# Three banks each for two kinds of attention scores, or two for one and four for the other

## The reference

```python
q = bitnet_linear(hidden_states, q_weight, q_scale)      # 32 heads of 32
k = bitnet_linear(hidden_states, k_weight, k_scale)      # 8 heads of 32, each used by 4 query heads
v = bitnet_linear(hidden_states, v_weight, v_scale)
scores = jnp.einsum('bhqd,bhkd->bhqk', q, k) / np.sqrt(HEAD_DIM)
attn = jax.nn.softmax(scores, axis=-1)
out = jnp.einsum('bhqk,bhkd->bhqd', attn, v)
...
x = x + bitnet_linear(out, o_weight, o_scale) + ffn(xn)
```

## Time and profile before

| | |
|---|---|
| median of 3 runs | 2635.26 us (2633.21 to 2635.6) |
| the profiled execution, its own time | 2635.6 us |
| its span in the trace | 2633.6 us |
| attention, from the first row scores to the last pair sums | about 315 to 1289 us |
| mean granted clock of PE over the span | 0.962 of full speed |
| busy: PE, DVE, ACT, POOL | 92%, 69%, 59%, 37% of the span |

### The profile page before, as it was taken

The page is one execution under the profiler, slowest core; times in us unless marked ns, Lnnn a source line. Parts: engine busy times, 40 slices in busy tenths (PEclk is TensorE's granted clock), DMA queues, the critical chain, the costliest instruction groups (busy, mean ns, idle before and its releaser), DMA issues.

```text
span 2633.6 us, 33630 instructions
## 1 busy us (share of the span) xinstructions
PE 2421.2 (92%) x12408; PEld 968.9 (37%) x12408; DVE 1828.4 (69%) x2362; ACT 1559.0 (59%) x1988; POOL 983.0 (37%) x545
## 2 busy tenths in 40 slices
PE   2499899989999999999689999999999999999998
PEld 1344322222222222222234444444444444444444
DVE  6756687766676767666154777777777777777777
ACT  3633267766676777667512666666666566666664
POOL 1000058788787888879600112122000112122000
PEclk9799889999999999999789999999999999999999
DMA  5100045544545455455412111112111311012211
GB/s 165 64 4 33 22 79 81 87 68 74 75 75 83 69 80 72 74 79 73 102 68 92 33 32 49 32 42 98 45 41 64 128 32 49 32 47 101 101 41 64
DMA packets 173711, 174.65 MB, mean 66 GB/s; under 512 B 87587, under 2 KB 119203, under 8 KB 173559
## 3 DMA queue, kind: packets, MB, share of 16 engines
q1 hardware_dynamic: 111286, 150.62, 18.2%
q0 software_dynamic: 62272, 22.03, 10.9%
HBM read 160.08 MB, written 65.45 MB: 86 GB/s over the span
## 4 chain that ended last, share of the span: by engine, by line
PE 54%; POOL 8%; issue 6%; DVE 1%; ACT 1%; DMA 1%; SPq 0%; DVEq 0%; POOLq 0%; ACTq 0%
PE ps L1309 29%; PE ps L1325 15%; POOL zone L504 6%; PE ps L1289 4%; PE ps L1212 2%; PE ps L1201 1%; POOL dequantised L525 1%; PE ps L1224 1%; PE ps L1185 1%; POOL zone L513 1%; PE ps L1341 0%; DMA zone<-in_L_attn_o_weight_dram 0%; ACT zone L657 0%; DVE zone L1098 0%; POOL zone L508 0%
## 5 line engine op out<-in xcount | busy, mean ns | idle before, releaser
L934 DVE TENSOR_REDUCE zone<-ps 128x1 f32<-128x512 f32 x1024 | 639.6, 683 | 271.5 <-PE ps L1185 271.3
L657 ACT ACTIVATE zone<-ps,sm 128x512 f32<-128x512 f32 x1024 | 631.6, 690 | 267.2 <-PE ps L1201 170.5
L1309 PE MATMUL ps<-xT,zone 128*128 128x512 f16 x3584 | 774.6, 379 | 3.6 <-DVE zone L1098 2.8
L504 POOL TENSOR_TENSOR zone<-zone 128x1024 f32<-128x1024 f32 x256 | 649.7, 2689 | 69.9 <-ACT zone L657 41.0
L1075 DVE TENSOR_SCALAR ps<-ps,zone_c 128x1024 f32<-128x1024 f32 x392 | 506.8, 1293 | 161.1 <-PE ps L1309 159.2
L725 ACT ACTIVATE ps<-ps,zone_c 128x1024 f32<-128x1024 f32 x392 | 426.8, 1089 | 261.1 <-PE ps L1309 259.3
L1309 PEld LDWEIGHTS ps<-xT,zone 128*128 128x128 f16 x3584 | 350.1, 98 | 427.4 <-DVE zone L1098 4.2
L1201 PE MATMUL ps<-zone 98*128 98x512 f16 x1024 | 392.9, 387 | 55.7 <-ACT zone L657 55.7
L1185 PE MATMUL ps<-zone 96*128 96x512 f16 x1024 | 405.2, 397 | 11.3 <-DMA zone<-zone 10.5
L1325 PE MATMUL ps<-zone 128*128 128x512 f16 x1792 | 387.1, 379 | 0.0
L1086 DVE TENSOR_SCALAR ps<-ps,zone_c 128x1024 f32<-128x1024 f32 x216 | 279.3, 1293 | 93.0 <-PE ps L1325 92.9
(11 more groups left out here) (127 smaller groups left out, 1292.6 us busy)
## 6 DMA issues: line engine op xcount, KB each, us to landing
zone<-dequantised SPq DMA_DIRECT2D x84, 512.0 KB, 3.6
dequantised<-zero_points SPq DMA_DIRECT2D x84, 256.0 KB, 4.1
zone<-zone SPq DMA_DIRECT2D x384, 32.0 KB, 2.3
zone<-_attn_hidden_states_dram SPq DMA_DIRECT2D x16, 512.0 KB, 6.8
zone<-inverse_sums SPq DMA_DIRECT2D x128, 64.0 KB, 2.5
attention<-zone SPq DMA_DIRECT2D x32, 256.0 KB, 2.0
xT<-attention SPq DMA_DIRECT2D x4, 2048.0 KB, 12.0
dequantised<-in_L_ffn_gate_w_dram POOLq DMA_DIRECT2D x28, 256.0 KB, 6.4
```

Of the source, the lines that this page charges most:

```text
L504: nc.gpsimd.tensor_tensor(duo[n % 3], prob[:, e % 8, :], prob[:, (e + 2) % 8, :], add).then_inc(s["sum_ok"], 1)
L657: A(prob[:, e % 8, m % 2 * 512:(m % 2 + 1) * 512], ps[:, 3 + m % 3, :], ACT.Exp, scale=gam[:, 0:1]).then_inc(s["exp_ok"], 1)
L934: V.tensor_reduce(mxs[:, u % 2, half, i % 16:i % 16 + 1], ps[:, (2 * i + half) % 3, :], AX, amax).then_inc(s["max_ok"], 1)
L1309: last = MM(ps[:, 4 * s2 + 2 * m + c, :], ring[:, buf, m * H + g * P:m * H + (g + 1) * P], xT[:, hf, part, g, c * 512:(c + 1) * 512], star ...
```

## The change

Of the six PSUM banks for scores, the row scores get two instead of three (the first half of the keys always bank 0, the second half bank 1), and the key scores get four, as two pairs (banks 2, 3 and 4, 5). The two key matmuls of a step then go out together, one step further ahead: in step e PE sends the pair of step e + 2. One exponential takes both banks. The semaphore counts follow: `st_pe` and `exp_ok` now count steps and not halves. The maxima are split into two float16 numbers before the transpose, on 128 partitions (`split_max`), so that the transpose is one of float16 and `copy_rows` is one copy.

```diff
-                sp.wait_ge(s["st_pe"], 32 * u + 32)
+                sp.wait_ge(s["st_pe"], 16 * u + 16)
...
-                pool.wait_ge(s["exp_ok"], 2 * (e + 3))
+                pool.wait_ge(s["exp_ok"], e + 3)
...
             def exp_step(e):
+                act.wait_ge(s["st_pe"], e + 1)
                 if e >= 8:
...
-                for m in (2 * e, 2 * e + 1):
-                    act.wait_ge(s["st_pe"], m + 1)
-                    A(prob[:, e % 8, m % 2 * 512:(m % 2 + 1) * 512], ps[:, 3 + m % 3, :], ACT.Exp,
-                      scale=gam[:, 0:1]).then_inc(s["exp_ok"], 1)
+                A(prob[:, e % 8, :].rearrange("p (a c) -> p a c", a=2), ps[:, 2 + 2 * (e % 2):4 + 2 * (e % 2), :],
+                  ACT.Exp, scale=gam[:, 0:1]).then_inc(s["exp_ok"], 1)
...
             exp_step(0)
+            exp_step(1)
             for e in range(STEPS):
                 u, k = e // 16, e % 16
-                if e + 1 < STEPS:
-                    exp_step(e + 1)
-                if k == 1 and u:
+                if e + 2 < STEPS:
+                    exp_step(e + 2)
+                if k == 0 and u:
                     evacuate_values(u - 1)
...
-                    V.tensor_reduce(mxs[:, u % 2, half, i % 16:i % 16 + 1], ps[:, (2 * i + half) % 3, :], AX, amax).then_inc(s["max_ok"], 1)
-
-            def top_max(u):
+                    V.tensor_reduce(mxs[:, u % 2, half, i % 16:i % 16 + 1], ps[:, half, :], AX, amax).then_inc(s["max_ok"], 1)
+
+            def split_max(u):
                 dve.wait_ge(s["max_ok"], 32 * u + 32)
-                V.tensor_reduce(mtop, mxs[:, u % 2, :, :].rearrange("p h c -> p c h"), AX, amax).then_inc(s["top_ok"], 1)
-
-            def split_rows(u):
+                m = mxs[:, u % 2, 0, :]
+                ch.inc(V.tensor_tensor(m, m, mxs[:, u % 2, 1, :], amax))
+                settle()
+                ch.inc(V.tensor_scalar(mhl[:, 0:16], m, -1.0 / MU, None, mult))
+                settle()
+                V.scalar_tensor_tensor(mhl[:, 16:32], m, -1.0 / MU, mhl[:, 0:16], mult, sub).then_inc(s["mhl_ok"], 1)
+
+            def copy_rows(u):
                 dve.wait_ge(s["m_pe"], u + 1)
-                m = ps[0:16, 7, 0:P]
-                ch.inc(V.tensor_scalar(mrow[:, u % 2, 0, :], m, -1.0 / MU, None, mult))
-                settle()
-                V.scalar_tensor_tensor(mrow[:, u % 2, 1, :], m, -1.0 / MU, mrow[:, u % 2, 0, :], mult, sub).then_inc(s["mrow_ok"], 1)
+                V.tensor_copy(mrow[0:32, u % 2, :], ps[0:32, 7, 0:64].bitcast(f16)).then_inc(s["mrow_ok"], 1)
...
-                c = 2 * i + half
-                if c >= 3:
-                    pe.wait_ge(s["max_ok"], c - 2)
-                MM(ps[:, c % 3, :], qst[0:96, u % 3, i % 16 // 4, i % 4 * P:(i % 4 + 1) * P],
+                if i:
+                    pe.wait_ge(s["max_ok"], 2 * (i - 1) + half + 1)
+                MM(ps[:, half, :], qst[0:96, u % 3, i % 16 // 4, i % 4 * P:(i % 4 + 1) * P],
                    kst[0:96, u // 2 % 2, half * 512:(half + 1) * 512], start=True, stop=True).then_inc(s["s_pe"], 1)
...
-                TR(ps[0:16, 7, 0:P], mtop, id32[:]).then_inc(s["m_pe"], 1)
-
-            def key_scores(m):
-                e, a = m // 2, m % 2
+                TR(ps[0:32, 7, 0:64].bitcast(f16), mhl[:, 0:32], id16[:]).then_inc(s["m_pe"], 1)
+
+            def key_scores(e):
                 u, kt, hp = e // 16, e % 16 // 2, e % 2
...
-                if m >= 3:
-                    pe.wait_ge(s["exp_ok"], m - 2)
-                MM(ps[:, 3 + m % 3, :], kst[0:98, u // 2 % 2, kt * P:(kt + 1) * P],
-                   qst[0:98, u % 3, 2 * hp + a, :], start=True, stop=True).then_inc(s["st_pe"], 1)
+                if e >= 2:
+                    pe.wait_ge(s["exp_ok"], e - 1)
+                for a in range(2):
+                    last = MM(ps[:, 2 + 2 * (e % 2) + a, :], kst[0:98, u // 2 % 2, kt * P:(kt + 1) * P],
+                              qst[0:98, u % 3, 2 * hp + a, :], start=True, stop=True)
+                last.then_inc(s["st_pe"], 1)
...
             for e in range(STEPS):
                 u, k = e // 16, e % 16
                 if e + LEAD < STEPS:
                     row_scores(e + LEAD, 0)
-                if 2 * e + 3 < 2 * STEPS:
-                    key_scores(2 * e + 3)
+                if e + 2 < STEPS:
+                    key_scores(e + 2)
                 if e + LEAD < STEPS:
                     row_scores(e + LEAD, 1)
-                if 2 * e + 4 < 2 * STEPS:
-                    key_scores(2 * e + 4)
```

More of the change, by code:

```diff
@@ L156, in layer_kernel @@
         mxs = zone_d[:, 0:64].rearrange("p (n h c) -> p n h c", n=2, h=2)
-        mtop = zone_d[:, 64:80]
+        mhl = zone_d[:, 64:80].bitcast(f16)
         ones = zone_d[:, 80:112]
@@ L190, in layer_kernel @@
         zone_c = sb("zone_c", [P, 736])
-        mrow = zone_c[0:16, 0:256].bitcast(f16).rearrange("p (n h c) -> p n h c", n=2, h=2)
+        zst = zone_c[:, 0:512].bitcast(f16).rearrange("p (n c) -> p n c", n=2)
+        mrow = zone_c[:, 512:640].bitcast(f16).rearrange("p (n c) -> p n c", n=2)
         tab = zone_c[:, 0:IT * 16].rearrange("p (t m g) -> p t m g", t=IT, m=2)
@@ L223, in layer_kernel @@
             kv_out q_in0 q_in1 q_in2 m_in0 m_in1 m_in2 k_in0 k_in1 v_in0 v_in1 const_ok
-            s_pe max_ok top_ok m_pe mrow_ok st_pe exp_ok pv_pe dn_pe sum_ok ev_ok evd_ok
+            s_pe max_ok mhl_ok m_pe mrow_ok st_pe exp_ok pv_pe dn_pe sum_ok ev_ok evd_ok
             dc_in0 dc_in1 rc_ok rs_out rb_in0 rb_in1 mu_ok oh_ok ol_ok
@@ L298, in load_m @@
                     sp.dma_start(qst[96 + part:97 + part, u % 3, :, :].rearrange("a h (q c) -> a (h q) c", q=4),
-                                 mrow[:, u % 2, part, :]).then_inc(s[f"m_in{u % 3}"], 16)
+                                 mrow[16 * part:16 * part + 16, u % 2, :]).then_inc(s[f"m_in{u % 3}"], 16)
             def store_kv(b):
@@ L930, in row_max @@
                 if i % 16 == 0 and u >= 2:
-                    dve.wait_ge(s["top_ok"], u - 1)
+                    dve.wait_ge(s["mhl_ok"], u - 1)
                 for half in range(2):
                     dve.wait_ge(s["s_pe"], 2 * i + half + 1)
-                    V.tensor_reduce(mxs[:, u % 2, half, i % 16:i % 16 + 1], ps[:, (2 * i + half) % 3, :], AX, amax).then_inc(s["max_ok"], 1)
-            def top_max(u):
+                    V.tensor_reduce(mxs[:, u % 2, half, i % 16:i % 16 + 1], ps[:, half, :], AX, amax).then_inc(s["max_ok"], 1)
+            def split_max(u):
                 dve.wait_ge(s["max_ok"], 32 * u + 32)
-                V.tensor_reduce(mtop, mxs[:, u % 2, :, :].rearrange("p h c -> p c h"), AX, amax).then_inc(s["top_ok"], 1)
-            def split_rows(u):
+                m = mxs[:, u % 2, 0, :]
[5 more added lines that the diff above has]
+            def copy_rows(u):
                 dve.wait_ge(s["m_pe"], u + 1)
-                m = ps[0:16, 7, 0:P]
-                ch.inc(V.tensor_scalar(mrow[:, u % 2, 0, :], m, -1.0 / MU, None, mult))
-                settle()
-                V.scalar_tensor_tensor(mrow[:, u % 2, 1, :], m, -1.0 / MU, mrow[:, u % 2, 0, :], mult, sub).then_inc(s["mrow_ok"], 1)
+                V.tensor_copy(mrow[0:32, u % 2, :], ps[0:32, 7, 0:64].bitcast(f16)).then_inc(s["mrow_ok"], 1)
             def invert(u):
@@ L953, in _ @@
                 if i == 15:
-                    top_max(0)
+                    split_max(0)
                 if i == 17:
-                    split_rows(0)
+                    copy_rows(0)
             for e in range(STEPS):
@@ L961, in _ @@
                 if k == 6 and u + 1 < UNITS:
-                    top_max(u + 1)
+                    split_max(u + 1)
                 if k == 7 and u + 1 < UNITS:
-                    split_rows(u + 1)
+                    copy_rows(u + 1)
                 if k == 12 and u:
@@ L1181, in row_scores @@
                         pe.wait_ge(s[f"k_in{u // 2 % 2}"], 48 * (u // 4 + 1))
-                c = 2 * i + half
-                if c >= 3:
-                    pe.wait_ge(s["max_ok"], c - 2)
-                MM(ps[:, c % 3, :], qst[0:96, u % 3, i % 16 // 4, i % 4 * P:(i % 4 + 1) * P],
+                if i:
+                    pe.wait_ge(s["max_ok"], 2 * (i - 1) + half + 1)
+                MM(ps[:, half, :], qst[0:96, u % 3, i % 16 // 4, i % 4 * P:(i % 4 + 1) * P],
                    kst[0:96, u // 2 % 2, half * 512:(half + 1) * 512], start=True, stop=True).then_inc(s["s_pe"], 1)
             def maxima_rows(u):
-                pe.wait_ge(s["top_ok"], u + 1)
+                pe.wait_ge(s["mhl_ok"], u + 1)
                 if u >= 2:
                     pe.wait_ge(s["evd_ok"], u - 1)
-                TR(ps[0:16, 7, 0:P], mtop, id32[:]).then_inc(s["m_pe"], 1)
-            def key_scores(m):
-                e, a = m // 2, m % 2
+                TR(ps[0:32, 7, 0:64].bitcast(f16), mhl[:, 0:32], id16[:]).then_inc(s["m_pe"], 1)
+            def key_scores(e):
```

(14 more changed lines are left out.)

## The result

The changed kernel takes 2818.31 us (median of four runs, 2809.23 to 2826.05), against 2635.43 before: a ratio of 1.069, interval 1.066 to 1.073. I had forecast 2645, with a range up to 2662. The change costs 183 us where I had 10. The profiled execution spans 2821.0 us at a mean clock of 0.934.

A forecast was written before the change was run, and what follows sets the result against it. PE was taken to bound the kernel, by its flow or by the chain behind the inverse sums, whichever is longer. Lead +5, first two units +4, steady part +1, last units 0: +10 us on 2635.6, about 2645, range 2628 to 2662.

The forecast's parts named there:

- the one on the maxima: DVE between bursts: three small operations replace one, some 0.4 us more, offset by other savings; together 0 (-0.1 to +0.3) a unit.
- flow: A unit's time when PE has no stall: 26.44 us before, forecast 29.1 us with eight bubbles of 0.33.
- signs of being wrong: Prediction wrong if the fourth matmul waits, C moves because transfers fall otherwise, or POOL, busy 81%, becomes late.
- The bubble: In each PE burst the third row matmul waits for its bank: d = 0.29 us, taken as 0.33, eight a unit.
- The exponential: On ACT, one of about 1.09 us replaces two of 0.69; release at the blocked matmul comes 0.4 us later.
- The chain behind the inverse sums: Last key scores, query transfers, inverse sums, POOL, ACT, PE restart: mean C 17.75 us, stalling PE once a unit.
- The steady part without the split: 27 units, 409 to 1215 us: 29.9 us each against 29.85, five stalls totalling 9.3 us left; +1 us in all.
- the faster rival: Bubble at its lower bound, remaining stalls too short to lower the clock (mean 0.99 or more): 2626 us; chance 0.18.
- The lead: 25 steps of row scores alone before the units: 0.2 us more a step, +5 us; first two units add +4.
- changes nothing: Rival: bubble hidden in the stall, lead's loss made up by an earlier T; within 5 us of 2635; chance 0.24.
- The second bubble: Rival: each burst's fourth row matmul waits too, or releases cost a weight load; d 0.5 to 0.6, 2665 us; chance 0.12.
- the clock: Rival: PE's pauses in every burst keep it at 1.2 GHz a tenth of the time, 40 us: 2685; chance 0.03.

The follow-up runs named there:

- experiment 1: Changed kernel with the maxima done as before (one reduction, float32 transpose, split reading PSUM); banks, pairs and wide exponential stay: 2634.51 us, ratio 0.9995.
- experiment 4: Changed kernel with POOL's pair additions cut from 1024 to 64 columns, leaving out most of the denominators: 2604.58 us, ratio 0.988.
- Experiment 3: Kernel before with only the row scores put in two banks; key scores, exponentials and maxima as before: 2670.69 us, ratio 1.014.
- experiments 6 and 7: Inverse sums sent before the query transfers: 6 on the changed kernel with the old maxima, 2613.89 us; 7 on the kernel before, 2548.57 us.
- the probe: Kernel before with eight small DVE operations of different kinds added per unit on spare memory: 2751.27 us, one run alone.
- experiments 2 and 8: 2: kernel before with only the new split of the maxima, 2775.73 us; 8: changed kernel with the halves joined by a reduction, 2779.24 us.

## Why the prediction was wrong, point by point

**The step that failed** is the one on the maxima: "three small DVE operations where `top_max` had one of 0.19, some 0.4 us more", "together 0 (-0.1 to +0.3 a unit)". I took the price of the three from `top_max` and never asked what POOL does at that moment. It was busy 653 of 806 us. `top_max` is a reduction, and a reduction takes 0.19 us beside POOL too: in the kernel before it began during an operation of POOL's in 25 of 32 units and never took more than 0.19. So the row I went by could not have shown the wait. Measured, the three are 5.48 us a unit. PE waits 4.4 of it at the transpose. The unit of 35.88 is 28.7 of flow, 4.4 of this wait and 2.8 of the clock behind it (0.72 for 10 us). The old stall is gone: PE's idle time before key matmuls that wait for ACT is 0.2 us in all from 409 to 1400 us. With the step undone (experiment 1) nothing is left of the loss. The bound of +0.3 had no reason but the size of the operands. None of my signs of being wrong named this wait; I had named POOL as what might become late, but not what DVE does beside it.

**The bubble** was right: d = 0.29 by the rows. In the changed kernel the third row matmul is 1.18 behind the first, and the flow, which experiment 4 lays bare, is 28.70 us: 26.44 + 8 x 0.28. My 0.33 was too much; the fourth matmul isn't late. Experiment 3 shows that without the pairs it would be, and a burst 3.30.

**The exponential** was right: 1.11 us (1.113 in the mean) against 1.09, and the later release at the blocked matmul too. Before, PE restarts 0.74 us behind the start of ACT's instruction (711.02 to 711.76), in experiment 1 1.17 us (716.44 to 717.61): 0.43 later, where I had 0.4.

```profile
711.02 1.27 ACT L657 ACTIVATE zone<-ps,sm 128x512 f32<-128x512 f32 x2 [4.42 <-issue]
```

```profile
716.44 1.11 ACT L656 ACTIVATE zone<-ps,sm 128x1024 f32<-128x1024 f32 x1 [3.73 <-POOL zone L504]
```

```profile
717.61 0.60 PE L1200 MATMUL ps<-zone 98*128 98x512 f16 x2 [2.58 <-ACT zone L656]
```

That ACT's spared time is worth nothing, as it had idle time before, no run tests by itself.

**The chain behind the inverse sums** was right, shown by experiments 6 and 7.

**The steady part without the split** was +1 us by my sum, and experiment 1 has a unit of 29.53 against 29.95: 26 x -0.42 = -11 us. The flow alone, 28.70 where I had 29.1, is as much. The stalls came as reckoned: five of over 0.7 us from 409 to 1215 us, 11.5 us of waiting in all with the short ones, where I had five with 9.3. Behind three of them the next 10 us had clock 0.83, 0.83 and 0.71, behind two (1.0 and 1.7 us) 1.00. The clock was 0.99 from 420 to 1150 us, against 0.96, the condition that I had named for the faster rival. **The lead** was +5 by my sum; its 32 reductions take 22.19 us in place of 19.23, which is 0.19 a step. Lead and first two units together came to 9.6 us by the second store of experiment 1 (431.77 against 422.18), where I had 9. The two terms nearly cancel, which is luck, and experiment 1 stands 2 us from the kernel before. The rest of the change would have been my "changes nothing", not the forecast.

**The rivals.** None of mine was the one that came. The second bubble and the clock were wrong as causes. The clock fell as a consequence of PE's wait: it was 1.00 ahead of each wait, and in experiment 4, which has PE's pauses in every burst but not this wait, it is 1.00 from 420 to 1150 us.

## What to carry to other kernels

Before moving a small operation to DVE, look at what POOL runs at that moment, and where the operands lie. With its main operand in PSUM, or as a reduction, it costs its size; with two operands in SBUF, or as a copy or scaling within SBUF, it waits for POOL's running instruction, once for each operation, and at times for the next one too (up to 6.0 us in the changed kernel). A stall that recurs at the same place hides small costs in front of it, so a part that seems free may cost its full price once the stall is removed: two banks for the row scores, with the pairs, cost nothing here, and 65 us after the transfers were reordered.

## What the runs showed of the hardware

A DVE operation that waits for POOL is recorded as busy, not as idle, from its start to the end of the wait. It may wait for more than one instruction of POOL: L940 from 819.20 to 823.76 outlasted both additions of 818.43 to 823.72, and the probe's copy took 14.28 us once.

```profile
817.63 1.42 POOL L526 DMA_DIRECT2D dequantised<-in_L_ffn_up_w_dram  x1
818.43 5.29 POOL L505 TENSOR_TENSOR zone<-zone 128x1024 f32<-128x1024 f32 x2
```

```profile
819.20 4.56 DVE L940 TENSOR_TENSOR zone<-zone 128x16 f32<-128x16 f32 x1
```

Whether it gets in between two additions, as at 568 us, or not, as here, goes with what POOL did ahead of them. Here POOL issues a transfer (L526) right before the first addition, and the records of the two additions overlap: 2.99 and 2.97 us long, started 2.3 us apart. At 568 us no transfer is issued there, and the records of 2.34 and 2.33 us stand end to end. In the changed kernel and experiments 2 and 8 a waiting DVE operation met the meeting point of two additions 94 times. Where the transfer's issue stood right ahead, it outlasted both, 27 of 27 times; where it didn't, it got in between, 67 of 67 times. In the probe the overlapping records decide in the same way in all 77 cases, with the transfer's issue sometimes further ahead. No run moves these issues, so that the cause isn't shown.
